# Scaling and splitting the SSM input projection's weights in the first expert loop, and re-timing the steps of the scan stage

## The reference

```python
x = x + attention_a(_layernorm(x), Wq, Wdkv, Wkr, Wukv, Wo)
x = x + ffn(_layernorm(x), W1, b1, W2, b2, W3, b3, Wg, bg)      # 8 experts, top 2
x = x + attention_b(_layernorm(x), W_in, conv_w, conv_b, A_log, D, dt_bias, norm_w, W_out, mup_vector)
x = x + ffn(_layernorm(x), ...)                                  # the same weights again

# attention_b, an SSM: 64 heads of 8 channels, state 128
proj = hidden_states @ W_in * mup_vector                         # 256 x 1344
z, xBC, dt = split(proj, [512, 512 + 768])
xBC = silu(conv_b + causal convolution of 4 taps of xBC);  x, B, C = split(xBC)
dt = softplus(dt + dt_bias);  dA = exp(dt * -exp(A_log))
state = state * dA + (dt * x) (outer) B;  y = state @ C          # a scan over 512 tokens
out = rmsnorm((y + D * x) * silu(z)) * norm_w @ W_out
```

## Time and profile before

| what | us |
|---|---|
| median of 3 runs (1450.88 to 1454.97) | 1452.22 |
| the profiled execution | 1456.39 |
| its span, first to last instruction | 1454.5 |
| PE busy in it | 1177.6 (81%) |
| DVE busy | 980.0 (67%) |
| ACT busy | 638.3 (44%) |
| POOL busy | 615.7 (42%) |

### The profile page before, as it was taken

One profiled execution on the slowest core, in us unless ns is written; L12 is line 12 of the kernel. 1 busy time (PEld: TensorE's weight loads), 2 busy tenths in 40 slices (PEclk: granted clock), 3 DMA queues, 4 the chain that ended last, 5 costly groups with the idle time before them and its releaser, 6 DMA issues. The chain is left out here.

```text
span 1454.5 us, 32135 instructions
## 1 busy us (share of the span) xinstructions
PE 1177.6 (81%) x12288; PEld 887.3 (61%) x12288; DVE 980.0 (67%) x2086; ACT 638.3 (44%) x1497; POOL 615.7 (42%) x538
## 2 busy tenths in 40 slices
PE   2789898998864699999627985998989648999992
PEld 1356566665653498988613552665756437998881
DVE  6489798897877455555486847677687574555555
ACT  4366676676653133333345662343333223333341
POOL 0245455545430233333130295688796313333221
PEclk9899999999985699999958997899999859999996
DMA  4655756657523698665130002000000049966625
GB/s 157 156 133 157 179 157 174 162 161 174 155 83 88 235 423 304 255 218 215 64 137 8 25 14 47 13 17 2 2 2 1 16 101 397 420 232 246 252 91 184
DMA packets 96010, 212.87 MB, mean 146 GB/s; under 512 B 28721, under 2 KB 66866, under 8 KB 89714
## 3 DMA queue, kind: packets, MB, share of 16 engines
q1 hardware_dynamic: 86258, 188.26, 40.0%
q0 software_dynamic: 7488, 20.46, 4.0%
q10 hardware_dynamic: 2112, 2.10, 0.4%
HBM read 154.94 MB, written 38.54 MB: 133 GB/s over the span
## 5 line engine op out<-in xcount | busy, mean ns | idle before, releaser
L1226 ACT ACTIVATE ffn_h<-ffn_bank,ffn_b 128x256 f32<-128x256 f32 (+1 forms) x384 | 144.1, 430 | 276.1 <-PE ffn_bank L118 263.4
L1403 DVE CAST ffn_hh<-ffn_h 128x512 f16<-128x512 f32 (+1 forms) x192 | 73.7, 384 | 180.4 <-ACT ffn_h L1226 172.1
L1038 POOL DMA_INDIRECT ffn_xs<-xn_rows,ffn_from_rows x78 | 77.9, 998 | 264.7 <-PE ffn_bank L1121 178.8
L116 PE MATMUL ffn_bank<-ffn_hh,ffn_W 128*128 128x256 f16 (+1 forms) x768 | 180.8, 254 | 6.1 <-DVE ffn_hl L1405 6.0
L117 PE MATMUL ffn_bank<-ffn_hl,ffn_W 128*128 128x256 f16 (+1 forms) x768 | 180.7, 253 | 0.0
L118 PE MATMUL ffn_bank<-ffn_hh,ffn_W 128*128 128x256 f16 (+1 forms) x768 | 180.6, 253 | 0.0
L644 ACT ACTIVATE att_prob<-att_bank,att_nmax 128x512 f32<-128x512 f32 (+3 forms) x256 | 127.1, 525 | 29.5 <-DVE att_nmax L726 28.2
L733 DVE TENSOR_TENSOR att_ptl<-att_bank,att_pth 128x384 f16<-128x384 f32 (+1 forms) x192 | 114.2, 595 | 34.4 <-ACT att_pth L651 34.4
L651 ACT ACTIVATE att_pth<-att_bank 128x384 f16<-128x384 f32 (+1 forms) x192 | 101.4, 528 | 80.2 <-PE att_bank L591 80.2
L2129 ACT ACTIVATE ssmh_windows<-ssml_dtx 64x64 f32<-64x64 f32 x256 | 64.8, 253 | 152.2 <-PE ssm_Y L2028 144.9
L1045 POOL DMA_INDIRECT y_rows<-ffn_y,ffn_to_rows x78 | 76.8, 985 | 129.1 <-DVE ffn_y L1414 99.2
(11 more groups left out here) (355 smaller groups left out, 3251.9 us busy)
## 6 DMA issues: line engine op xcount, KB each, us to landing
ffn_W<-split_w SPq DMA_DIRECT2D x46, 2048.0 KB
att_piece<-in_ffn_w SPq DMA_DIRECT2D x32, 512.0 KB, 5.2
split_w<-att_halves SPq DMA_DIRECT2D x32, 512.0 KB, 4.3
att_Q<-att_pair SPq DMA_DIRECT2D x64, 128.0 KB, 2.4
ffn_back<-y_rows SPq DMA_DIRECT2D x16, 512.0 KB, 6.1
att_KB<-att_krl SPq DMA_DIRECT2D x8, 512.0 KB, 5.5
att_Q<-att_pair SPq DMA_DIRECT2D x64, 64.0 KB, 2.1
xn_rows<-ffn_XN SPq DMA_DIRECT2D x8, 512.0 KB, 2.6
```

The lines of the kernel that those rows point to most:

```text
L116: pe.matmul(out, ah, bh, start=start, stop=False)
L1226: ins_ = act.activation(h[layer][:, m, 0:n], bank[1 + 2 * layer + u][:, (m % 2) * n:(m % 2 + 1) * n], ACT.Gelu, bias=bias[:, ds(e + m, 1)])
```

## The change

In words. (1) W_in and mup_vector are laid out on the host with 64 zero columns on either side of dt's 64 (PAD = 1472 columns). (2) A class `SplitProjection` runs inside ffn1's loop in four parts of 128 x 736. SP loads a part and its piece of mup; POOL multiplies after its scatter of tile 2, 10, 15 and 20; ACT makes the high half between the two layers' Gelus in the body of tile 4, 12, 17 and 22; POOL makes the low half after the scatter of tile 5, 13, 18 and 23; SP stores both halves in DRAM (`split_in`) and waits for it before it loads the next part. After the last tile's weights SP does `store(2)`, `load(3)`, `store(3)` and waits until all is stored; its waits for the tiles' rows and the loads back come behind that. (3) ln2 loads the two halves as float16 and has no work of POOL and ACT on them. (4) The projection reads dt's columns with zeros beside them straight from these halves. (5) D * x of batch 2 goes from POOL in the projection to ACT in the heads (p = 24, 26, 28, 30). (6) In the heads `ident8` is one copy from the one-hot table; 12 groups of `picks` come after scan 1; batch 0's updates come one step later, block 0 and 1 of Y open one step later; of the fades of batches 1 to 3 the even chunks go from POOL to DVE, and POOL does the odd ones ahead of its multiply of the same step; `outputs` comes one step earlier for batches 0 to 2, and the addition to X stays where it was.

```diff
@@ ffn_stage: sync, in the loop and behind it; gpsimd and scalar in the loop
+                if beside is not None:
+                    beside.sync(sp, j)
+            if beside is not None:
+                beside.sync(sp, NTILE)
...
                 scatter(j)
+                if beside is not None:
+                    beside.gpsimd(pool, j)
...
                 gelus(1, j)
+                if beside is not None:
+                    beside.scalar(act, j)
                 if ahead >= 1:
                     gelus(0, j + 1)
@@
+class SplitProjection:
+    PARTS, COLS = 2 * KD, PAD // 2
+    SCALED_AT, HIGH_AT, LOW_AT = (2, 10, 15, 20), (4, 12, 17, 22), (5, 13, 18, 23)
...
+    def load(self, sp, i):
+        k, cols = self.part(i)
+        if i:
+            sp.wait_ge(self.stored, 32 * i)
+        sp.dma_start(self.w[:, :], self.w_in[k * P:(k + 1) * P, cols]).then_inc(self.loaded, 16)
+        sp.dma_start(self.m[:, :], self.mup[cols].unsqueeze(0).broadcast_to([P, self.COLS])).then_inc(self.loaded, 16)
+
+    def store(self, sp, i):
+        k, cols = self.part(i)
+        sp.wait_ge(self.low, i + 1)
+        sp.dma_start(self.split[0, :, k, cols], self.hi[:, :]).then_inc(self.stored, 16)
+        sp.dma_start(self.split[1, :, k, cols], self.lo[:, :]).then_inc(self.stored, 16)
+
+    def sync(self, sp, j):
+        if j == 8:
+            self.load(sp, 0)
+        if j in (14, 20):
+            i = (j - 14) // 6
+            self.store(sp, i)
+            self.load(sp, i + 1)
+        if j == NTILE:
+            self.store(sp, 2)
+            self.load(sp, 3)
+            self.store(sp, 3)
+            sp.wait_ge(self.stored, 32 * self.PARTS)
+
+    def gpsimd(self, pool, j):
+        if j in self.SCALED_AT:
+            i = self.SCALED_AT.index(j)
+            pool.wait_ge(self.loaded, 32 * (i + 1))
+            pool.tensor_tensor(self.w[:, :], self.w[:, :], self.m[:, :], ALU.mult).then_inc(self.scaled, 1)
+        if j in self.LOW_AT:
+            i = self.LOW_AT.index(j)
+            pool.wait_ge(self.high, i + 1)
+            pool.tensor_tensor(self.lo[:, :], self.w[:, :], self.hi[:, :], ALU.subtract).then_inc(self.low, 1)
+
+    def scalar(self, act, j):
+        if j in self.HIGH_AT:
+            i = self.HIGH_AT.index(j)
+            act.wait_ge(self.scaled, i + 1)
+            act.activation(self.hi[:, :], self.w[:, :], ACT.Copy).then_inc(self.high, 1)
@@ class SsmWeights
-        sp.dma_start(self.w, ins["ssm_W_in"].rearrange("(k p) n -> p k n", p=P)).then_inc(self.w_loaded, 16)
-        sp.dma_start(self.mup, ins["ssm_mup_vector"].unsqueeze(0).broadcast_to([P, PROJ])).then_inc(self.w_loaded, 16)
...
+        sp.dma_start(self.wih[:, :, :], self.split[0]).then_inc(loaded, 16)
+        sp.dma_start(self.wil[:, :, :], self.split[1]).then_inc(loaded, 16)
...
-            act.activation(self.wih[:, k, :], self.w[:, k, :], ACT.Copy).then_inc(self.high_split, 1)
...
-            pool.tensor_tensor(self.w[:, k, :], self.w[:, k, :], self.mup, ALU.mult).then_inc(self.scaled, 1)
...
-            pool.tensor_tensor(self.wil[:, k, :], self.w[:, k, :], self.wih[:, k, :], ALU.subtract)
@@ ssm_project_stage
-            pe.wait_ge(s["wd_ready"], 1)
...
-                    w = slice((1 - bb) * SH, (3 - bb) * SH)
+                    w = slice(SD + CONV + (1 - bb) * SH, SD + CONV + (3 - bb) * SH)
...
-            dve.memset(wdh[:, :, :], 0.0)
-            link(dve.memset(wdl[:, :, :], 0.0))
-            dve.tensor_copy(wdh[:, :, SH:2 * SH], wih[:, :, PROJ - SH:PROJ])
-            dve.tensor_copy(wdl[:, :, SH:2 * SH], wil[:, :, PROJ - SH:PROJ]).then_inc(s["wd_ready"], 1)
...
-                if n in (TB, 2 * TB):
-                    scale_x(n // TB)
+                if n == TB:
+                    scale_x(1)
@@ ssm_heads_stage
-        updates = {c: (0, c) for c in range(NC - 1)}
-        inters = {at: (0, q) for q, at in enumerate((7, 10, 13, 15))}
+        updates = {c + 1: (0, c) for c in range(NC - 1)}
+        inters = {at: (0, q) for q, at in enumerate((8, 10, 13, 15))}
...
-            inters |= {PAIRS_B * b + at: (b, q) for q, at in enumerate((-2, 2, 6, 10))}
+            inters |= {PAIRS_B * b + at: (b, q) for q, at in enumerate((-2, 2, 6, 9))}
...
-        opens = {0: 0, 1: 1, 4: 2, 14: 3} | ...
-        outputs = {PAIRS_B * b + (42 if b + 1 < B else 41): b for b in range(B)}
+        opens = {1: 0, 2: 1, 4: 2, 14: 3} | ...
+        outputs = {PAIRS_B * b + 41: b for b in range(B)}
...
-                if p in (40, 42, 44, 46):
+                if p in (24, 26, 28, 30, 40, 42, 44, 46):
...
-            for par in range(2):
-                rows = slice(par * CH, (par + 1) * CH)
-                dve.tensor_copy(ident8[rows, :].rearrange("p (c n) -> p c n", n=CH),
-                                identf[rows, rows].unsqueeze(1).broadcast_to([CH, 2 * TB, CH])).then_inc(ident_made, 1)
-            dve.tensor_scalar(pick(4, SH // 4), hot(4, SH // 4), UNSCALE, None, ALU.mult).then_inc(picks_made, 1)
+            dve.tensor_copy(ident8[:, :].rearrange("p (c n) -> p c n", n=CH), one_hot.unsqueeze(1).broadcast_to([P, NC, CH])).then_inc(ident_made, 1)
...
                 if p < NP:
                     scan(p)
+                if p == 1:
+                    dve.tensor_scalar(pick(4, SH // 4), hot(4, SH // 4), UNSCALE, None, ALU.mult).then_inc(picks_made, 1)
...
-                if p in updates and updates[p][0] == 0 and updates[p][1]:
+                if p in updates and updates[p][1] and (updates[p][0] == 0 or updates[p][1] % 2 == 0):
                     fade(*updates[p])
...
-                if p - 3 in outputs:
-                    add_output(outputs[p - 3], 0)
-                if p - 5 in outputs:
-                    add_output(outputs[p - 5], 1)
+                if p - 4 in outputs:
+                    add_output(outputs[p - 4], 0)
+                if p - 6 in outputs:
+                    add_output(outputs[p - 6], 1)
... (gpsimd)
+                if p in updates and updates[p][0] and updates[p][1] % 2:
+                    fade(*updates[p])
                 if p < NP:
                     mult(p)
-                if p in updates and updates[p][0] and updates[p][1]:
-                    fade(*updates[p])
```

76 lines of the change are left out of this document (41 added, 35 removed).

## The result

The changed kernel takes **1442.7 us** (median of 8 runs, 1436.9 to 1448.7) against 1452.4 of the kernel before on the same chip (8 runs): ratio **0.9929, 95% interval 0.9905 to 0.9953**, 9.7 us less. On another chip the same kernel later gave 0.9954 (0.9934 to 0.9975). I had forecast 1443.2, 9.05 us less. The profiled execution took 1445.6 us, its span is 1443.9.

The account below looks back on a forecast made before the run. No single engine bounds the kernel: PE is busy 81%, and barriers close stages in which different engines end last. Gains of 15.75 less costs of 6.7 give 9.05 us less, a median of 1443.2, range 1437 to 1451.5.

Parts of the forecast that it names:

- ln2 and the projection's start: ln2 to the projection's first matmul: without POOL's multiplies and ACT's splits, a gain of 6.15 us (5.5 to 8.2).
- ffn1's loop: New work in ffn1's narrow tiles: POOL's operations hold DVE's casts, cost 2.5 us; ACT's copies delay Gelus, cost 1.3 us.
- SP: In ffn1's loop SP's waits between weight loads are covered by loading 8 tiles ahead: cost 0, upper bound 1.5 us.
- ffn1's end: After the last scatter, the loads back wait for a subtraction and stores: cost 2.4 us (1.5 to 3.5).
- Heads' start: Start of the heads: one ident copy and later picks let scan 0 start sooner, gain 2.0 us (0 to 4).
- Update phases: Heads' update phases: fewer fades on POOL save 0.4 us per four steps; gain 4.5 us, bounds loss 3, gain 11.
- Output product: Heads: the product one step earlier lets DVE scan instead of wait, only behind batch 2; gain 1.5 us (0 to 3).
- the hidden loop: Rival: ffn1's loop hides all of the new work, only the end's 2.4 us stays; time 1439.4, chance 0.17.
- full price everywhere: Rival: POOL's hold on DVE costs full price in ffn1's loop and the heads; time 1460.2, chance 0.08.
- late loads: Rival: ln2 still ends late because its new loads land after 761, losing 5 us; time 1448.2, chance 0.04.
- idle heads: Rival: the heads' edits give nothing, as waits for one engine replace waits for another; time 1450.7, chance 0.2.
- Nearly all of PE's idle time: Rival: the heads' update phases give 10 us for 4.5, nearly all of PE's idle time; time 1437.7, chance 0.09.

Follow-up runs that it names:

- the experiment: Changed kernel with two multiplications of 128 x 1344 put back on POOL in ln2, on other data, without the loads and ACT's splits: 1447.0 us, ratio 0.9956.
- parts_in_wide_tiles: Changed kernel with the split's POOL and ACT work moved to wide tiles, part 0 loaded ahead of the loop, final wait behind the loads back: 1439.1 us, ratio 0.9908.
- heads_undone: Changed kernel with all four edits of the heads' order undone, the weights' part kept: 1450.9 us, ratio 0.9982.
- after_again: The changed kernel, unchanged, measured again on another chip: 1446.6 us, ratio 0.9954.
- heads_only: Kernel before with the four edits of the heads' order alone put in: 1449.6 us, ratio 0.9964.
- wide_again: The kernel of parts_in_wide_tiles, measured again on one chip with after_again: 1439.1 us, ratio 0.9890.

## Why the prediction was right, point by point

- **ln2 and the projection's start**, 6.15: right, 6.6 measured. L188 and L193 are free, ACT's chain is what ends last. DVE's last instruction ends 18.35 us after the stage's start where I had laid out 18.9. That the hold made 4.6 of it rests on the rows of before; the experiment shows a hold, of 3.1.
- **Projection's end**, 1.6: right, 1.3 at the end itself and 1.7 in the kernel that undid it.
- **ffn1's loop**, 2.5 for POOL and 1.3 for ACT: the mechanism was right (parts_in_wide_tiles takes the whole cost away), the sum came close on average (3.1 measured for 3.8, partly by luck, as 0.9 of relief in tile 15 is in it), and one step failed: "They start when POOL's scatter is issued". I took the scatter to go out at once behind the output. Behind tile 15 it waits about 5 us for earlier scatters' landing, as it already did for 3.9 in the trace before, and so the multiply meets DVE elsewhere, at 2 us or at nothing. The terms of 0.9 and 0.7 behind tiles 20 and 18, where no scatter is late, were 0.6 and 0.5.
- **SP**, 0: right for the end result, and missed in one place. Part 0's two loads, issued at 511, landed 32 and 33 us later, behind five loads of 2 MB and beside a sixth, and POOL waited 7.9 us for them before its multiply at 544.68. Counted from the outputs, the two gathers behind it went out some 6 us later than before and the scatters of tiles 3, 4 and 5 went out 4.8, 5.6 and 2.0 us later. No output up to tile 5 came later for it, and tile 6 took 0.2 us more. So the slack of the wide tiles hid it, and not the eight tiles' lead that I had argued with.
- **ffn1's end**, 2.4: the mechanism was right, the size is 1.8, by the stores' landing.
- **Heads' start**, 2.0: right by both kernels that undo it, 2.0 and 1.9 at scan 16. The changed kernel shows 3.8 there against the kernel before; the other 1.8 is also in heads_undone, which has none of the start's edit, and goes together with PE's clock, though no run tries whether the clock is its cause: between 27 and 40 us of the stage, windows of 1 us show it short of full by 5.1 us in sum before and by 3.4 in heads_undone.
- **Update phases**, 4.5: right, 5.8 measured, less 1.7 given back between them. My mark for it was wrong: "POOL under 30 of 31 us in the phases". The engine that bounds stays full; what falls is the work for each step, and the steps in the window rise from 18 to 19.
- **Output product**, 1.5: 1.1 measured, but "this counts only behind batch 2" failed. It counts behind batch 0.
- **ACT's scalings**, 0.5: nothing (204.3 us from scan 16 to 127 with and without them).
- **Not in the sum**: the tail's 1.5 us, lost to the granted clock in this execution and not in after_again's. Here it offset part of the phases' surplus and the start's. The total came out within 1 us of the median partly by such offsets; term by term the errors are 0.3 to 1.8 us.

Of the rivals, the hidden loop is refuted (3.1 us paid), as is full price everywhere (wide tiles pay 0.2 us in the changed kernel, and the phases gain), late loads (none in ln2) and idle heads (5.2 us by heads_only, with an interval of 2.8 to 7.7, clear of nothing gained). Nearly all of PE's idle time was not had: 5.8 of 11.

## What to carry to other kernels

Work put beside a loop should be priced by where it falls in each tile's chain, not by its length. The same eight instructions cost 3 us with half of them in tiles without slack and 1 us with all of them in wide tiles, so moving them to other tiles was worth more than any of the forecast's finer points. A final wait belongs behind the issues that don't need it. For an engine that stays full before and after, count steps per window.

## What the runs showed of the hardware that I had not expected

- **The granted clock turned small waits of PE into larger losses, and not by the same amount each time.** A run of matmuls takes 1.89 us at half clock for 1.09, an output product 6.59 for 3.69; seven unused matmuls in a wait of 1.5 us kept the clock full and saved 3 us against the kernel beside it. Ahead of the fall in the changed kernel's tail PE had waited for 0.39 and 1.49 us, and was busy for 1.43 of the 3.0 us from 1127 to 1130. The same two waits, within 0.02 us, stand there in all thirteen profiles without the filling; the clock fell to half in each, and the product took 5.2 to 5.4 us in five of them and 5.9 to 6.6 in eight. Half clock doesn't always cost: the changed kernel's first profile has it for 3.4 us between scans 80 and 96, after_again not at all, and the stretch takes 25.9 us in both.
- **A hold can hit an instruction that the record has starting first.** The subtraction L1414 has its start at 673.84, 0.65 us ahead of POOL's multiply at 674.49, and would have ended at 674.27; it ended at 676.52, 0.29 behind the multiply. In heads_undone and after_again it is a cast, 0.45 and 0.39 us ahead, that takes 2.35 and 2.30. The twelve traces that have such operations draw one line. Where an operation of SplitProjection on POOL stands directly behind a scatter or gather, the 20 casts and subtractions of this kind on DVE that start 0.02 to 0.65 us ahead of its recorded start are all held until it ends (they end 0.16 to 0.56 us behind it), and the 28 that start 0.73 to 1.37 us ahead run their normal 0.3 to 0.8 us. The four instructions that read a PSUM bank beside one SBUF tile are free at 0.01 and 0.50 us too. The scatter alone isn't enough: of 1576 casts and subtractions that start during other scatters and gathers, in all fourteen traces, none takes over 1 us. Nor is the start alone: where POOL had waited 0.58 us behind its scatter (wide_again, 559.37), a subtraction 0.32 us ahead ran its 0.69 us and the multiply took 1.97 us for 1.75. So behind an indirect DMA POOL's operation holds DVE from about 0.7 us before its recorded start. Why it does so isn't shown.
- **Equal stages vary between profiles**: heads 267.0 to 270.0 us, ffn1's loop 56.1 to 60.4 with the same instructions. One profile doesn't price an effect of 2 us in these stages. The step from one tile or scan to the next does it better, once the same step is held against a second profile of the same code and against the granted clock in it.
